# A transformer block pair with sparse attention: the output projection put into the odd scores' bank, and the router's steps spread wider

## The reference, cut to what matters

```python
out = einsum('bhlk,bhlkd->bhld', attn, v) ...        # per block of 16 queries
y = out @ W_out                                      # output projection
x1 = layernorm(x + y)
logits = x1 @ w_router; probs = softmax(logits)      # 32 experts
top1 = argmax(probs); gate = probs[top1]
pos = cumsum(onehot(top1), axis=0)[row, top1] - 1    # running count over all rows
accepted = pos < 80; slot = top1 * 80 + pos          # row of x1 in the experts' buffer
```

## Time and profile before

| | us |
|---|---|
| median of 3 runs | 978.63 (976.86 to 981.81) |
| profiled execution, its own time | 980.25 |
| its span, first to last instruction | 978.4 |
| PE busy (matmuls) | 897.1 |
| DVE busy | 680.8 |
| ACT busy | 484.0 |
| POOL busy | 482.5 |
| mean granted PE clock | 0.908 |

### The profile page before, as it was taken

The page is one execution under the profiler, slowest core; times in us unless marked ns, Lnnn a source line. Parts: engine busy times, 40 slices in busy tenths (PEclk is TensorE's granted clock), DMA queues, the critical chain, the costliest instruction groups (busy, mean ns, idle before and its releaser), DMA issues.

```text
span 978.4 us, 17766 instructions
## 1 busy us (share of the span) xinstructions
PE 897.1 (92%) x5939; PEld 543.2 (56%) x5939; DVE 680.8 (70%) x2043; ACT 484.0 (49%) x1337; POOL 482.5 (49%) x508
## 2 busy tenths in 40 slices
PE   6878999999999999999999999999999888979784
PEld 3334566666666565666666656666658433535352
DVE  2779879697788886888897798832122466686863
ACT  4446645473547657658575575565313143244230
POOL 4564757776503677777775736775000622202110
PEclk8768999898989989999997898897899997999897
DMA  7210322112100111111111111155026200000000
GB/s 240 48 38 13 57 53 46 37 32 46 37 2 12 25 31 31 28 31 31 28 30 21 30 19 23 31 129 144 3 76 165 51 0 0 1 1 11 11 12 11
DMA packets 57721, 39.97 MB, mean 41 GB/s; under 512 B 25408, under 2 KB 48672, under 8 KB 57504
## 3 DMA queue, kind: packets, MB, share of 16 engines
q1 hardware_dynamic: 40608, 21.82, 8.6%
q0 software_dynamic: 14336, 15.72, 8.3%
q10 hardware_dynamic: 2688, 1.31, 0.5%
HBM read 33.31 MB, written 5.54 MB: 40 GB/s over the span
## 4 chain that ended last, share of the span: by engine, by line
PE 69%; DVE 14%; issue 6%; ACT 6%; DMA 2%; POOL 1%; SPq 1%; DVEq 0%; POOLq 0%; ACTq 0%
PE psK L600 7%; PE psX L777 7%; PE psI L614 6%; PE psK L703 5%; PE psP L760 4%; PE psK L691 4%; PE psS L734 3%; PE psS L1660 3%; PE psS L737 3%; PE psP L600 3%; PE psP L767 3%; PE psP L749 3%; DVE G L1835 2%; DVE idxf L1097 2%; PE psM L676 1%
## 5 line engine op out<-in xcount | busy, mean ns | idle before, releaser
L580 POOL DMA_INDIRECT G<-key_rows,idx x368 | 360.0, 978 | 214.1 <-issue 106.3
L982 ACT ACTIVATE PT<-psP 128x256 f32<-128x256 f32 x128 | 48.8, 381 | 164.3 <-PE psP L767 157.8
L600 PE MATMUL psK<-cst 128*128 128x512 bf16 x350 | 106.9, 419 | 3.3 <-ACT KT L958 3.3
L614 PE MATMUL psI<-kiT,qiT 64*128 64x512 f32 (+5 forms) x320 | 93.3, 606 | 8.9 <-ACT R L854 8.9
L958 ACT ACTIVATE KT<-psK 96x512 f32<-96x512 f32 x104 | 60.8, 585 | 44.6 <-PE psK L691 44.2
L1065 DVE SCALAR_TENSOR_TENSOR SC<-R,w_i,SC 128x512 f32<-128x512 f32 (+5 forms) x120 | 78.1, 651 | 6.7 <-ACT R L854 3.8
L1258 DVE CUSTOM_DVE_ANT_0 S<-psS,cst 128x208 f32<-128x208 f32 x128 | 47.0, 367 | 50.7 <-PE psS L737 50.7
L1095 DVE MAX8 top<-SC 128x8 f32<-128x128 f32 (+15 forms) x64 | 78.4, 1226 | 2.3
L1097 DVE FIND_INDEX8 idxf<-top,SC 128x8 uint32<-128x128 f32 (+15 forms) x64 | 78.2, 1221 | 0.0
L950 ACT ACTIVATE PR<-PR,rinv 128x208 f32<-128x208 f32 x128 | 58.2, 454 | 36.6 <-DVE rinv L1266 36.5
L854 ACT ACTIVATE R<-psI 128x512 f32<-128x512 f32 (+5 forms) x160 | 71.2, 493 | 9.0 <-PE psI L614 9.0
(11 more groups left out here) (336 smaller groups left out, 1826.1 us busy)
## 6 DMA issues: line engine op xcount, KB each, us to landing
G<-key_rows,idx POOLq DMA_INDIRECT x368, 2.5
rtmp<-idx_rows SPq DMA_DIRECT2D x24, 128.0 KB, 3.1
xslots<-zrow SPq DMA_DIRECT2D x4, 320.0 KB, 9.3
SC<-xslots SPq DMA_DIRECT2D x8, 160.0 KB, 2.5
yslots<-SC ACTq DMA_DIRECT2D x8, 160.0 KB, 2.9
V<-val_rows SPq DMA_DIRECT2D x15, 80.0 KB
xr<-in_x SPq DMA_DIRECT2D x1, 1024.0 KB, 9.4
qiT<-in_w_gate SPq DMA_DIRECT2D x4, 256.0 KB, 4.5
```

The source lines that it names most:

```text
L580: pool.indirect_dma_start(ring[o % RING][:, g % GPB, DR:], None, key_rows, bass.IndirectOffsetOnAxis(ap=idx[:, t, g:g + 1], axis=0),).then ...
L600: pe.matmul(ps[:, :].rearrange("p (a n) -> p a n", a=2), warm_w, warm_x, start=True, stop=True, skip_group_check=True)
L614: pe.matmul(psI[i][:, 0:w], lhs, kiT[64 * i:64 * i + 64, CH * c:CH * c + w], start=True, stop=True).then_inc(s["i_mm"], 1)
```

## The change

The projection of a tile is issued inside `scores`, ahead of the scores of the tile's successor's last block (b = 7; this falls in the same block step as before). It writes to PY, columns 384 to 512 of psS[1], and PE waits for it (y_mm) before it writes these scores. Only the last tile's projection is issued in the loop. On DVE the add of the inputs (`add_inputs`) comes straight behind `s_minimum` at b = 1, the statistics (`row_stats`) stay at the end of b = 1, and `normalize` goes to the front of b = 3. Transpose goes from b = 3 to 5, x1's copies from 4 to 6, the router from 5 to 7; routing goes from b = 6 to b = 0 of the next tile, the exponential from 6 to 1, cumulating from 7 to 1 and placing from 7 to 2. The loop gets three more steps. The waits on `s_min` and `vs_cp` in `scores` now stand ahead of those on `k_ev` and `q_cp`, and the scores of b = 1 wait for the add that empties PY. Query steps and the index plan are the same.

```diff
--- before.py
+++ after.py
@@ -110,7 +110,7 @@
     return sum(chunks_of(u) for u in range(t))
 
 
-N0, N1 = -2 * NB, NT * NB + 2 * NB
+N0, N1 = -2 * NB, NT * NB + 2 * NB + 3
 INDEX_END = NB * (NT - 2) - -1
 START_ROOM = 1.1
 TOP_STEPS = 12
@@ -373,6 +373,7 @@
         psI = [ctx.enter_context(nc.psum_tensor(f"psI{i}", [P, CH], F32)) for i in range(2)]
         psM = ctx.enter_context(nc.psum_tensor("psM", [P, CH], F32))
         PX = psX[:, 0:P]
+        PY = psS[1][:, 3 * P:4 * P]
 
         names = """ld_cst ld_tab ld_x ld_x2 ld_w ld_raw ld_late zeroed zslots kv_mm
             w_mm w_cp kproj kproj_cp rope_p lat_row key_l mu lrot kr_out val_out g_rot lT lT_cp rope rope_a
@@ -720,12 +721,17 @@
 
                 def scores(n):
                     t, b = divmod(n, NB)
-                    pe.wait_ge(s["k_ev"], n + 1)
-                    pe.wait_ge(s["q_cp"], 2 * t + 2)
                     if n >= 2:
                         pe.wait_ge(s["s_min"], n - 1)
                     if n >= 2 and (n - 2) // NB in ONE_HOT:
                         pe.wait_ge(s["vs_cp"], hot_order(n - 2) + 1)
+                    if b == 1 and t >= 2:
+                        pe.wait_ge(s["bn"], 3 * (t - 2) + 1)
+                    if b == NB - 1 and t >= 1:
+                        out_project(t - 1)
+                        pe.wait_ge(s["y_mm"], t)
+                    pe.wait_ge(s["k_ev"], n + 1)
+                    pe.wait_ge(s["q_cp"], 2 * t + 2)
                     if t in ONE_HOT:
                         values_transpose(n)
                     ps = psS[n % 2]
@@ -771,14 +777,16 @@
 
                 def out_project(t):
                     pe.wait_ge(s["o_cp"], NB * (t + 1))
+                    if t == NT - 1:
+                        pe.wait_ge(s["bn"], 3 * t)
+                    for h in range(NH):
+                        mm = pe.matmul(PY, OT[:, t % 2, :, :, h].rearrange("p b q -> p (b q)"), w_vo[:, h, :],
+                                       start=(h == 0), stop=(h == NH - 1), skip_group_check=True)
+                    mm.then_inc(s["y_mm"], 1)
+
+                def x1_transpose(t):
                     if t >= 1:
                         pe.wait_ge(s["rte"], t)
-                    for h in range(NH):
-                        mm = pe.matmul(PX, OT[:, t % 2, :, :, h].rearrange("p b q -> p (b q)"), w_vo[:, h, :],
-                                       start=(h == 0), stop=(h == NH - 1), skip_group_check=True)
-                    mm.then_inc(s["y_mm"], 1)
-
-                def x1_transpose(t):
                     pe.wait_ge(s["x1_n"], t + 1)
                     pe.transpose(PX, x1[:, t % 4, :], ident).then_inc(s["x1_t"], 1)
 
@@ -830,15 +838,15 @@
                             q_transpose(st + 1, 1)
                     if 0 <= st + 2 < NT and b == 7:
                         q_project(st + 2)
+                    if n == NB * (NT + 1):
+                        out_project(NT - 1)
                     if 0 <= st - 2 < NT:
-                        if b == 0:
-                            out_project(st - 2)
-                        if b == 3:
+                        if b == 5:
                             x1_transpose(st - 2)
-                        if b == 5:
+                        if b == 7:
                             router(st - 2)
-                        if b == 7:
-                            cumulate(st - 2)
+                    if 0 <= st - 3 < NT and b == 1:
+                        cumulate(st - 3)
                 second_tensor(pe)
 
             @block.scalar
@@ -1044,10 +1052,10 @@
                     if 0 <= st - 2 < NT:
                         if b == 2:
                             norm_scale(st - 2)
-                        if b == 4:
+                        if b == 6:
                             x1_copy(st - 2)
-                        if b == 6:
-                            gate_exp(st - 2)
+                    if 0 <= st - 3 < NT and b == 1:
+                        gate_exp(st - 3)
                 second_scalar(act)
 
             @block.vector
@@ -1265,9 +1273,11 @@
                         dve.wait_ge(s["p_nrm"], n - 1)
                     dve.reciprocal(rinv[:, n % 2:n % 2 + 1], psumr[:, n % 4:n % 4 + 1]).then_inc(s["orec"], 1)
 
-                def add_and_stats(t):
+                def add_inputs(t):
                     dve.wait_ge(s["y_mm"], t + 1)
-                    dve.tensor_tensor(xa[:, :], PX, xr[:, t, :], ALU.add).then_inc(s["bn"], 1)
+                    dve.tensor_tensor(xa[:, :], PY, xr[:, t, :], ALU.add).then_inc(s["bn"], 1)
+
+                def row_stats(t):
                     dve.wait_ge(s["bn"], 3 * t + 1)
                     dve.bn_stats(out=stats[:, 0, :], in_=xa[:, :]).then_inc(s["bn"], 1)
                     dve.wait_ge(s["bn"], 3 * t + 2)
@@ -1329,6 +1339,8 @@
                         g_rotate(n + 1)
                     if 0 <= n - LAG_M < NT * NB:
                         s_minimum(n - LAG_M)
+                    if b == 1 and 0 <= st - 2 < NT:
+                        add_inputs(st - 2)
                     if 0 <= n - LAG_R < NT * NB:
                         row_inverse(n - LAG_R)
                     if n == 1:
@@ -1343,8 +1355,10 @@
                         if b == 3:
                             q_rotate(st + 1, 1)
                     if 0 <= st - 2 < NT:
-                        if b == 6:
-                            route(st - 2)
+                        if b == 3:
+                            normalize(st - 2)
+                    if 0 <= st - 3 < NT and b == 0:
+                        route(st - 3)
                     for kind, t, i in index_steps.get(n, ()):
                         if kind == "sum":
                             combine(t, i)
@@ -1352,13 +1366,10 @@
                                 index_mask(t)
                         else:
                             topk_step(t, i)
-                    if 0 <= st - 2 < NT:
-                        if b == 1:
-                            add_and_stats(st - 2)
-                        if b == 2:
-                            normalize(st - 2)
-                        if b == 7:
-                            place(st - 2)
+                    if 0 <= st - 2 < NT and b == 1:
+                        row_stats(st - 2)
+                    if 0 <= st - 3 < NT and b == 2:
+                        place(st - 3)
                 second_vector(dve)
```

More of the change, by code:

```diff
@@ L773, in out_project @@
                     pe.wait_ge(s["o_cp"], NB * (t + 1))
-                    if t >= 1:
-                        pe.wait_ge(s["rte"], t)
+                    if t == NT - 1:
+                        pe.wait_ge(s["bn"], 3 * t)
                     for h in range(NH):
-                        mm = pe.matmul(PX, OT[:, t % 2, :, :, h].rearrange("p b q -> p (b q)"), w_vo[:, h, :],
+                        mm = pe.matmul(PY, OT[:, t % 2, :, :, h].rearrange("p b q -> p (b q)"), w_vo[:, h, :],
                                        start=(h == 0), stop=(h == NH - 1), skip_group_check=True)
@@ L781, in x1_transpose @@
                 def x1_transpose(t):
+                    if t >= 1:
+                        pe.wait_ge(s["rte"], t)
                     pe.wait_ge(s["x1_n"], t + 1)
```

## The result

The changed kernel takes 993.16 us (median of 4 runs, 990.45 to 996.18), the kernel before 978.58 in the same session: ratio 1.0146, interval [1.0102, 1.0189]. It is slower by 14.6 us. A second session with 6 and 11 runs gave 994.25 against 978.68, ratio 1.0159 [1.0128, 1.0191]. The forecast was 983.5 with a range up to 989, so the time lies outside it.

A forecast was written before the change was run, and what follows sets the result against it. The prediction took TensorE as what everyone waits for, its matmuls busy 897 of 978 us. Terms 3.5 + 0.7 - 0.5 + 1.2 = +4.9 us, against the median 978.63, gave 983.5, range 975 to 989.

The forecast's parts named there:

- The clock, "a spread and no sum": Clock falls after each projection; projection plus block-7 scores keep their joint length, so no direction, only +-5 us.
- the sign that I had named, a clearly different sum: Stated test: the prediction is wrong if the low-clock stretches sum to a clearly different length.
- The rival that the clock comes back sooner: Index matmuls behind the projection shorten low stretches in eight of 16 rounds: -13.6 us, about 970; chance 10%.
- The wait: TensorE waits for its own projection before the last block's scores, 15 times 0.23 us: +3.5 us (1.7 to 6.8).
- VectorE late (+0.7): Later block-7 scores delay VectorE's reduction in step 1, making TensorE wait 0 to 3 us once; 0.7 taken.
- The rival that VectorE becomes the bound: VectorE binds behind the late scores in step 1, +2 us in each of four more stretches: 991; chance 13%.
- Waits that go (-0.5): TensorE's waits for the placing (0.3 us) and partly for ScalarE's ReLU (0.2) vanish: -0.5 us (0 to -1.8).
- The tail (+1.2): After block 127, 6 more fill-in matmuls between last projection and transpose, mostly at the high clock: +1.2 us (0.5 to 2.5).

The follow-up runs named there:

- after: First trace of the changed kernel, with the whole change against the kernel before: execution 990.45 us, span 988.4.
- after_again: The changed kernel unchanged, run again in a second session: ratio 1.0159 to the kernel before; its trace has execution 995.09 us, span 993.3.
- order_only: Kernel before with the projection issued ahead of block 7's scores, in its old bank, without the wait or new hand-offs: 986.24 us, ratio 1.0080.
- bank_and_order: Kernel before with the projection's new order, bank and wait and the earlier add, but the router's old steps: 994.84 us, ratio 1.0168.
- wait_only: Kernel before plus only TensorE's wait for its own projection (y_mm), in the old place: 984.71 us, ratio 1.0044.
- one_head_before: Kernel before with one of the projection's 16 matmuls per tile, in a session where the kernel before took 1280 us: 1238.11 us.
- one_head_before_3: Kernel before with one of the projection's 16 matmuls per tile, in a session where the kernel before took 979.16 us: 929.84 us, ratio 0.9491.
- after_old_tail: Changed kernel with the old steps for the last tile's router, in a session of 1280 us: 1295.28 us, ratio 1.0100 to the kernel before.
- packed_before: Kernel before with weighted sums stored head by head, so projection weight loads read neighbouring numbers: 940.39 us, ratio 0.9593; ratios 0.9869 and 0.9851 in slow sessions.

## Why the prediction was wrong

**The clock, "a spread and no sum": this step failed.** I saw that the clock falls after each projection (in 11 of 15 rounds it falls within it), and reasoned that the projection and the scores keep their joint length, so no direction followed. What I missed is that the two do not pay alike. The projection takes 4.08 us at the full clock and 4.15 to 4.19 with up to 2.5 us of low clock inside: for it a low microsecond is nearly free. The rows for this stood in the trace of before. The work behind it pays 0.44 to 0.45 of every low microsecond. With scores and index matmuls behind it, low clock lay on the paid side instead of the free one: inside projections 17.4 us became 4.6 and 8.5, outside 78.2 became 90.9 and 93.9. That is +5.1 and +6.3 us in the blocks (6.4 and 7.9 at a half), where I had 0 +- 5. In `after` the sum of low clock did not change at all (95.6 and 95.5 us), so the sign that I had named, a clearly different sum, would have missed it; in `after_again` 6.8 us more of it came on top. Another 2.2 us were lost behind the scatter, with more low clock there, for a reason that stays open.

**The range.** The forecast left the clock's 5 us out of it, and its upper end was added wrongly: the upper bounds of the terms are 6.8 + 3 + 2.5 = 12.3, which above 978.63 is 991 and not 989. With the clock the stated terms reach 996.

**The rival that the clock comes back sooner** had the right place and the wrong sign: the index matmuls behind the projection did not shorten the low stretches, they sat in them (1.99 us instead of 1.06). The page of the Trainium skill that I weighed there ("TensorE: Matmul & The Clock Gate") lays such falls, in another section (HAM oscillation — how this bites in real kernels), to waits in which the engine idles. Here the row in which the clock of the kernel before falls (224 to 226 us) has TensorE recorded busy 2.00 of 2.00 us; a rule about idleness alone would miss it.

**The wait** came 15 times, as said, and cost 0.13 us, next to my lower bound of 0.11: 2.0 instead of 3.5. It was mis-sized by 1.5.

**VectorE late (+0.7)**: VectorE waits for the scores of block 7 in step 1, as forecast, and nothing of it reaches TensorE, which has no listed wait for it in the changed kernel. The rival that VectorE becomes the bound falls by these rows. (bank_and_order, which loses as much without the moved hand-offs, has the late scores too and so says nothing on this one.)

**Waits that go (-0.5)**: the one for the placing went (0.3); that for the ReLU grew from 1.5 to 2.2 and two small ones by 0.6. Together TensorE's waits grew by 1.0 us. But order_only and bank_and_order show that without the spreading an early projection waits 3.4 to 3.7 us for the placing, which I had not priced.

**The tail (+1.2)**: the 15 fill-ins ahead of the transpose are there. The chain of waits of `after` (start us, us, what):

```profile
716.58 4.11 PE psS L783 x16
720.68 1.39 PE psK L601 x3
...
722.77 4.13 PE psK L601 x12
...
727.00 1.29 PE psK L601 x6
728.30 0.14 PE psX L795 x2
728.44 1.29 PE psK L601 x6
...
```

From the last weighted sums to the scatter it is 2.7 and 2.8 us longer. The 15 cost 5.5 us, partly at the low clock, where the earlier trace rows had 3.43 for 9. I had assumed that most of the added ones would run at the full clock; the term came out above its upper bound of 2.5.

By measured terms, in the traces of `after` and `after_again`: waits 2.0 in both, clock in the blocks 5.1 and 6.3, rest of the blocks 1.3 and 1.2, tail 2.7 and 2.8, behind the scatter 2.2 and 2.3. That is 13.3 and 14.6 us, beside 14.6 between the medians.

## What to carry to other kernels

Before pricing a reordering, sort the work by what sets its pace: here the matmuls bound by strided weight loads took nearly the same time at either clock, so low clock that fell on them was free, and what was put behind them instead paid. Don't take that for granted of every load: the packed ones slowed with the clock. And ask what brings the clock down in the first place: here it was one small matmul group with a strided weight operand, and storing that operand in the order in which it is read was worth 4% where the order of the work was worth 1.5%. A sum that says "no direction" for the clock should be tested with the rows at hand, by comparing the same instruction inside and outside a low stretch.

## What the runs showed of the hardware

- A projection of 16 fp32 matmuls with a stride of 64 bytes in its weight loads (331 ns each) takes 4.08 us at the full clock, 4.15 with 2.5 us of low clock inside. Packed (187 ns each at the full clock) it takes 2.05 us, and 3.37 with 2.96 us of low clock inside. With the strided loads the clock falls in the projection or just behind it, though TensorE is busy all of the row; with one head in place of 16 it does not fall in twelve tiles.
- Of two kernels whose low clock is equal in sum (95.6 and 95.5 us), one is 8.4 us longer. Where the low clock lies counts as much as how much of it there is.
- Kernels differ in how their executions spread: wait_only falls in two groups 7 us apart, the kernel before in one (975 to 980, but for a few).
- In four sessions out of seven the kernel before took 979 us; in the three others every kernel took some 1240 to 1305 us. One chip had a session of each kind, with 1283 and 979 us. VectorE's, ScalarE's and POOL's busy times differ by about 2% at most (one_head_before against one_head_before_3: 679.8 and 678.6 us on VectorE); TensorE's are longer, 899.8 against 815.8, at a lower clock. TensorE then mostly stands still while POOL issues gathers, as in 200 to 230 us of one_head_before, with POOL busy 19.54 of 30:

```profile
200.00:230.00 30.00, 7.80 (x19) 3.06 (x18) 0.46 (x3) 0.53 (x2) 19.54 (x21) 0.50 0.12 24
```

The instruction durations are unchanged (a gather 0.95 us, the projection's loads 330 ns in after_old_tail), but ScalarE and VectorE wait for releasers that the trace calls remote, and TensorE's gaps have none. What holds them was not found. Kernels are closer to each other in such a session than in the others (packed_before 0.986 of the kernel before against 0.959).
